# A two-layer transformer block: folded query weights, split key tables and a fourth buffer of gathered rows in the sparse attention

## The chip, the cores and the metric

The kernel runs on one core of one Trainium2 chip. The metric is the device time of one execution in microseconds, the median of the runs given. The engines are named as the profile names them: PE (TensorE matmul), PEld (its weight loads), DVE (VectorE), ACT (ScalarE), POOL (GpSimd) and SP (SyncE, which here only issues DMAs).

## The reference, cut to what matters

A sequence of 2048 rows of 128 values passes four stages, each added to the residual: a dense attention, a mixture of 16 experts, a sparse attention, and a shared expert with 8 hashed ones. Only the third is changed. Its inputs are in fact used for one sequence of 2048 rows, with at most 96 keys for each query row:

```python
c_kv = x @ W_dkv                                   # 2048 x 32
I = sum_h relu(q_i @ k_i.T) * idx_w                # index scores, 4 heads
# of row t: the last 64 keys always, later keys never, and of the rest the best
_, idx = jax.lax.top_k(I, 96)                      # 64 near keys, then 32 far ones
key_c = (c_kv @ W_uk)[idx];  value = (c_kv @ W_uv)[idx]
c_q = x @ W_dq                                     # 2048 x 64
query_c = c_q @ W_uq                               # 8 heads x 64
query_r = rotate(softplus(c_q @ W_qr))             # 8 heads x 32, angle by row
key_r = rotate(softplus((x @ W_kr)[idx]))          # angle by place in idx
attn = softmax((query_c . key_c + query_r . key_r) * scale)
out = (attn . value) @ W_out
```

## The kernel before

The rows are cut into 16 tiles of 128 (t = 0 to 15). The sparse attention, `layer1_attention`, has two blocks of instructions, and between two blocks all engines meet: none starts the next block before all have ended this one.

**The first block, `projections1`.** DVE normalizes the rows. PE then works through a list `jobs`, in a ring of four PSUM banks; each job fills one bank and ACT (for some jobs DVE) empties it. The kinds are `xnT` (four transposes of normalized rows), `kv` (the 64 numbers of each key: 32 of c_kv and 32 for the rotation), `ki` and `qi` (index keys and queries, kept as a high and a low half, the low one computed by DVE), `cq` (the 64 numbers c_q of each row), `wqq` (W_uq and W_uk folded for each head), `q` (one tile of all heads' queries, from c_q and `wqq`), `nout` (W_uv and W_out folded) and `near` (transposes of the rotated keys). Between jobs, `begin` and `finish` mark where a softplus starts and ends, and `scored` where the index scores of the first three tiles are computed and ranked (`first_score`, `first_rank`). DVE's `new_keys` adds the keys' softplus to `rows`, SP copies all of `rows` to the table `key_table` in HBM, and POOL, once the table is there and a tile is ranked (`place_ready`), gathers the far keys: each indirect DMA fetches 128 rows of 64 numbers, tile 0 has 16 of them and every other tile 32 (`gathers`). In this block POOL issues those of tiles 0 and 1, on line 1137.

**The second block, `selected_attention`.** The order of the work on PE, ACT and DVE is written out in slots by `selected_schedule`, eight slots a tile; `index_schedule` spreads the index scores and the ranking of the tiles 3 to 15 over the slots, and `A_SLOT` says how many slots the scoring of tile 0 starts behind them. Each tile needs, in this order: its gathered keys rotated in two halves on DVE (`keys`; first instruction on line 1041), their transposes on PE and copies on ACT (`far`), scores, softmax, and the context sums on PE, which read the gathered rows themselves (line 1746), then the product with `nout` and the addition to x (line 1668). `spin` rotates the queries of two tiles, on DVE with `angle` tables that SP loads; unit 0 stands at the start of this block. POOL runs on its own:

```python
for t in range(GATHERED, NT):
    m = t % RING
    pool.wait_ge(place_ready, t + 1)
    if t >= RING:
        pool.wait_ge(ctx_full, 2 * (t - RING + 1))
    for i in range(32):
        pool.indirect_dma_start(far[m][:, i, :], ...)
```

So a tile's gathers wait until the tile is ranked, and until the context sums of the tile `RING` before it, which held the same buffer, are done. A row's place list lies in one of six buffers (`PLACES`).

## Time and profile before

| what | value |
|---|---|
| median of 3 runs | 2347.01 us (2346.33 to 2355.41) |
| the profiled execution | 2350.25 us, its span 2348.5 us |
| projections, first to second meeting of the engines | 1500.9 to 1608.7 us |
| second block of the sparse attention | 1608.7 to 2281.9 us |
| PE busy over the span | 91% |
| POOL busy over the span | 78% |

The times of the views are microseconds from the start of the span. The profiled execution took 3.24 us more than the median of the runs, and 1.75 us of it lie outside its span. What happens before 1500.9 us and after 2281.9 us is the work of the other three stages.

### The profile page before, as it was taken

The numbers are of one execution on the slowest core, as the hardware profiler recorded it, in microseconds if no ns is written. First come the engines' busy times: TensorE is split into PE (matmuls) and PEld (weight loads), VectorE is DVE, ScalarE is ACT, GpSimd is POOL, SyncE is SP. The second block draws the span as 40 slices with busy tenths as digits, with TensorE's granted clock in tenths as the row PEclk, the third lists the DMA queues.
The fourth block names the chain that finished last, engine by engine and source line by source line (L and its number), as shares of the span: only waits on it lengthen the run. The fifth ranks groups of instructions, "written<-read, shape, count | busy, mean of one in ns | idle before, by whom it ended". The sixth has DMA issues, their size and how long they took to land. (4 is left out here: it accounts for less than half of the span.)

```text
span 2348.5 us, 56810 instructions
## 1 busy us (share of the span) xinstructions
PE 2136.3 (91%) x22652; PEld 1279.2 (54%) x22652; DVE 1793.4 (76%) x3458; ACT 1718.3 (73%) x3500; POOL 1825.1 (78%) x1239
## 2 busy tenths in 40 slices
PE   5899999999999999999999689787999888887868
PEld 2466666666666666666666556533454444444434
DVE  7788888888888888888887379767788777775223
ACT  4898998989989989899899546445666756654433
POOL 4899999999999999999999547357177777777700
PEclk8999999999999999999999789865689998977769
DMA  4000000000000000000000001111111111111110
GB/s 147 1 2 2 2 2 2 2 2 2 2 2 2 2 2 2 2 2 3 2 2 2 15 13 27 47 28 32 30 33 38 38 31 38 33 31 35 32 29 18
DMA packets 44288, 43.19 MB, mean 18 GB/s; under 512 B 20912, under 2 KB 33024, under 8 KB 43776
## 3 DMA queue, kind: packets, MB, share of 16 engines
q0 software_dynamic: 15872, 16.28, 3.7%
q1 hardware_dynamic: 28160, 23.35, 3.5%
q8 instruction: 178, 2.92, 0.5%
q14 instruction: 78, 0.64, 0.1%
HBM read 33.83 MB, written 1.57 MB: 15 GB/s over the span
## 5 line engine op out<-in xcount | busy, mean ns | idle before, releaser
L380 POOL TENSOR_TENSOR probs_lo<-probs,probs_hi 128x1024 f16<-128x1024 f32 x512 | 1076.4, 2127 | 41.7 <-ACT probs L430 41.2
L494 DVE TENSOR_REDUCE part_max<-aux 128x1 f32<-128x512 f32 x1024 | 677.7, 686 | 90.8 <-PE aux L568 86.4
L429 ACT ACTIVATE probs_hi<-scores 128x512 f16<-128x512 f32 x1024 | 627.9, 613 | 133.4 <-PE scores L601 116.0
L430 ACT ACTIVATE probs<-scores 128x512 f32<-128x512 f32 x1024 | 633.4, 619 | 0.0
L1509 POOL DMA_INDIRECT far<-key_table,placeT x448 | 442.7, 988 | 189.4 <-issue 135.9
L617 PE MATMUL acc<-v,probs_hi 128*128 128x65 f16 x4096 | 451.6, 193 | 2.3 <-POOL probs_lo L380 2.3
L619 PE MATMUL acc<-v,probs_hi 128*128 128x64 f16 x4096 | 452.8, 195 | 0.0
L621 PE MATMUL acc<-v,probs_lo 128*128 128x65 f16 x4096 | 451.1, 192 | 0.0
L617 PEld LDWEIGHTS acc<-v,probs_hi 128*128 128x128 f16 x4096 | 382.8, 96 | 82.7 <-POOL probs_lo L380 2.6
L619 PEld LDWEIGHTS acc<-v,probs_hi 128*128 128x128 f16 x4096 | 380.3, 97 | 75.5
L568 PE MATMUL aux<-k_a,q_a 128*128 128x512 f16 x1024 | 392.6, 384 | 4.4 <-DVE roped L480 2.1
L600 PE MATMUL scores<-q_a,k_a 128*128 128x512 f16 x1024 | 388.7, 380 | 6.6 <-ACT probs L430 6.5
L601 PE MATMUL scores<-q_b,k_b 65*128 65x512 f16 x1024 | 389.6, 380 | 0.0
L621 PEld LDWEIGHTS acc<-v,probs_lo 128*128 128x128 f16 x4096 | 381.8, 99 | 0.0
L601 PEld LDWEIGHTS scores<-q_b,k_b 65*128 65x128 f16 x1024 | 100.1, 98 | 112.5 <-issue 0.2
L568 PEld LDWEIGHTS aux<-k_a,q_a 128*128 128x128 f16 x1024 | 100.1, 98 | 83.0 <-DVE part_max L494 13.8
L600 PEld LDWEIGHTS scores<-q_a,k_a 128*128 128x128 f16 x1024 | 100.3, 98 | 81.4 <-ACT probs L430 26.1
L846 POOL TENSOR_TENSOR e_hid_lo<-e_hid,e_hid_hi 128x512 f16<-128x512 f32 x64 | 74.1, 1159 | 63.4 <-ACT e_hid_hi L802 63.4
L1041 DVE TENSOR_TENSOR far_turned<-far,cos_far 128x512 f32<-128x512 f32 x31 | 21.6, 697 | 131.9 <-DMA far<-key_table,placeT 131.8
L1528 ACT ACTIVATE farT<-a_turn 128x512 f32<-128x512 f32 x64 | 38.2, 597 | 103.5 <-PE a_turn L1699 102.9
L472 DVE TENSOR_TENSOR rope_term<-aux,cos 128x512 f32<-128x512 f32 x128 | 88.5, 691 | 25.6 <-PE aux L551 22.5
L1723 PE MATMUL a_score<-near_keys,qT 64*128 64x256 f32 x256 | 105.3, 496 | 0.0
(319 smaller groups left out, 4083.3 us busy)
## 6 DMA issues: line engine op xcount, KB each, us to landing
far<-key_table,placeT POOLq DMA_INDIRECT x496
qT<-qT SPq DMA_DIRECT2D x16, 256.0 KB
e_w<-in_e_w SPq DMA_DIRECT2D x48, 64.0 KB, 1.9
x<-in_x SPq DMA_DIRECT2D x4, 256.0 KB, 3.9
cos<-in_cos SPq DMA_DIRECT2D x1, 1024.0 KB, 7.0
sin<-in_sin SPq DMA_DIRECT2D x1, 1024.0 KB, 9.0
e_w<-in_e_w SPq DMA_DIRECT2D x2, 512.0 KB, 4.1
out<-x SPq DMA_DIRECT2D x4, 256.0 KB, 2.7
```

The costliest lines, as they stand in the source:

```text
L380: pool.tensor_tensor(probs_lo[:, slot], probs[:, wide], probs_hi[:, slot], ALU.subtract).then_inc(low_ready, 1)
L429: act.activation(probs_hi[:, slot, i], bank, ACT.Exp, scale=float(DH0) ** -0.5)
L430: act.activation(probs[:, wide, i], bank, ACT.Exp, scale=float(DH0) ** -0.5).then_inc(probs_ready, 1)
L494: dve.tensor_reduce(part_max[g % 2][:, n % QT, n // QT:n // QT + 1], bank, AX.X, ALU.max).then_inc(aux_free, 1)
L568: ins = pe.matmul(bank, qa[g % QRING][:, t * P:(t + 1) * P], ka[h % 2][:, c * CH:(c + 1) * CH], start=True, stop=True)
L600: pe.matmul(out, ka[h % 2][:, keys], qa[g % QRING][:], start=True, stop=False)
L601: pe.matmul(out, kb[h % 2][:, keys], qb[g % QRING][:], start=False, stop=True).then_inc(scores_ready, 1)
L617: pe.matmul(out, probs_hi[:, n % SLOTS, i, queries], high, start=(kt == 0 and t == 0), stop=False, skip_group_check=True)
L619: pe.matmul(out[:, 0:DH0], probs_hi[:, n % SLOTS, i, queries], low, start=False, stop=False, skip_group_check=True)
L621: ins = pe.matmul(out, probs_lo[:, n % SLOTS, i, queries], high, start=False, stop=(kt == KT0 - 1), skip_group_check=True)
L1509: pool.indirect_dma_start(far[m][:, i, :], None, keep["table"], bass.IndirectOffsetOnAxis(ap=placeT[t % PLACES][:, i:i + 1], axis=0)).then ...
L1723: pe.matmul(b[:, 0:WIN], qT[t % 2][0:KW, 0, 4 * g:4 * g + 4].rearrange("k i a h -> k (i a h)"), near[:, t * P:t * P + WIN], start=False, s ...
```

## The change

In words, part by part:

- **Buffers.** `RING` is 4: there is a fourth buffer `far3`. It is paid for in memory by laying `nout` and the context sums `ctxT` on the 32 partitions beside the near keys (`BESIDE`), and by keeping `near_key` in `far3` during the first block.
- **POOL.** The first block issues the first 32 gathers only (16 of tile 0, 16 of tile 1) and reads a table of the first 1024 rows; the second block issues the other 464.
- **Key tables.** The keys are finished and written in two halves, each with its own softplus, and the near keys are rotated later, by `near_keys`.
- **Projections.** The four `cq` jobs go. One job `wall` multiplies W_dq into `wqq`, and each `q` job multiplies 128 rows of weights with the transposed x. `wqq` and `nout` come before the first `xnT`, behind six loads of their own (`fold_in`). ACT empties all `q` jobs (DVE emptied every other one). The list `after` says what follows which job.
- **First rotation.** `spin` 0 moves to the first block (`first_spin`), its `angle` loads with it.
- **Slots.** `A_SLOT` is 2.

```diff
-RING = 3
+RING = 4
 EARLY = 3
-GATHERED = 2
+FIRST_GATHERS = 2 * 16
+FIRST_ROWS = T // 2
 TOP_OPS = 3 * (FAR // 8)
+ANGLES = ("cos_q", "sin_q", "cos_near", "sin_near")
...
+        wdqT = sb("wdqT", [CQ, D], F32)
         wuq = sb("wuq", [DH1, H1, CQ], F32)
         wuk = sb("wuk", [DH1, H1, CKV], F32)
         wuv = sb("wuv", [DH1, H1, CKV], F32)
         wo = sb("a1_wo", [DH1, H1, D], F32)
...
-        wqq = sb("wqq", [CQ, H1 * CKV + NQ], F32)
+        wqq = sb("wqq", [CQ, H1, ROPE1 + CKV], F32)
+        wq_all = sb("wq_all", [P, H1 * (ROPE1 + CKV)], F32)
...
-        near_key = sb("near_key", [P, NT, KW], F32)
-        last_e, last_u = (part[:, NT - SOFT:].rearrange("p t h r -> p (t h r)") for part in (e, u))
+        near_key = keep["far"][RING - 1][:, 0:NT, :]
+        last_e = e[:, NT - SOFT:].rearrange("p t h r -> p (t h r)")
...
-        jobs = [("xnT", c) for c in range(NCH)] + [("kv", i) for i in range(2)]
+        folded = [(wuq, "wuq"), (wuk, "wuk"), (wuv, "wuv"), (wo, "a1_wo"), (wqq[:, :, 0:ROPE1], "wqr"), (wdqT, "wdqT")]
+        loads = [(wkvr, "wkvr"), (widxk, "widxk"), (widxq, "widxq"), (keep["idx_w"], "idx_w"),
+                 (keep["cap0"], "cap0"), (keep["cap"], "cap"), (cos_k, "cos_k"), (sin_k, "sin_k"),
+                 (keep["mask"], "mask_first"), (keep["unit"], "unit"), (keep["cos_far"], "cos_far"),
+                 (keep["sin_far"], "sin_far")]
+
+
+
         later = [i for i in range(NIDX * NCH) if i % NCH]
-        jobs += [("ki", 0)] + [("qi", NCH * h) for h in range(NIDX)] + [("ki", c) for c in range(1, NCH)]
-        jobs += [("cq", c) for c in range(NCH)] + [("wqq", 0)] + [("q", t) for t in range(NT)]
-        jobs += [("qi", i) for i in later]
-        jobs += [("nout", i) for i in range(2)] + [("near", c) for c in range(NCH)]
-        by_vector = lambda kind, i: kind in ("ki", "qi") or (kind == "q" and i % 2 == 1)
+        queries = lambda lo, hi: [("q", t) for t in range(lo, hi)]
+        jobs = [("wqq", 0), ("nout", 0), ("nout", 1), ("xnT", 0), ("ki", 0), ("qi", 0), ("xnT", 1), ("qi", NCH),
+                ("kv", 0), ("qi", 2 * NCH), ("qi", 3 * NCH), ("xnT", 2), ("xnT", 3), ("wall", 0), ("kv", 1), ("ki", 1)]
+        jobs += queries(0, 3) + [("ki", 2)] + queries(3, 8) + [("ki", 3)] + queries(8, NT)
+        jobs += [("qi", i) for i in later] + [("near", c) for c in range(NCH)]
+        by_vector = lambda kind, i: kind in ("ki", "qi")
...
+        after = {
+            ("kv", 0): [("begin", 0)],
+            ("qi", 3 * NCH): scores(0),
+            ("xnT", 3): [("finish", 0), ("rank", 0)],
+            ("kv", 1): [("begin", 1)],
+            ("ki", 1): scores(1) + [("finish", 1)],
+            ("q", 0): [("rank", 1)],
+            ("ki", 2): scores(2),
+            ("q", 3): [("begin", 2), ("rank", 2)],
+            ("q", 5): [("near", 0)],
+            ("q", 7): [("begin", 3)],
+            ("q", 8): [("finish", 2)],
+            ("q", 9): [("spin", 0)],
+            ("q", 11): [("begin", 4), ("finish", 3)],
+            ("q", 15): [("begin", 5)],
+            ("qi", later[2]): [("finish", 4)],
+            ("qi", later[6]): [("finish", 5)],
+        }
...
+                for dst, src in folded:
+                    sp.dma_start(dst if isinstance(dst, bass.AP) else dst[:], dram[src]).then_inc(fold_in, 16)
                 for dst, src in loads:
-                    sp.dma_start(dst if isinstance(dst, bass.AP) else dst[:], dram[src]).then_inc(w_in, 16)
-                sp.wait_ge(keep["rows_ready"], 1)
-                sp.dma_start(keep["table"].rearrange("(t p) d -> p t d", p=P), rows[:]).then_inc(keep["table_out"], 16)
-                sp.wait_ge(keep["table_out"], 16)
+                    sp.dma_start(dst[:], dram[src]).then_inc(w_in, 16)
+                for k in range(2):
+                    for j, n in enumerate(ANGLES):
+                        sp.dma_start(angle[k][:, j], dram[n][:, SPIN * k:SPIN * k + SPIN, :]).then_inc(angles_in[k], 16)
+                for k in range(2):
+                    sp.wait_ge(rows_ready, k + 1)
+                    sp.dma_start(keep["table"][k * FIRST_ROWS:(k + 1) * FIRST_ROWS, :].rearrange(
+                        "(t p) d -> p t d", p=P), rows[:, of_keys(k), :]).then_inc(table_out[k], 16)
+                for k in range(2):
+                    sp.wait_ge(table_out[k], 16)
...
-                pool.wait_ge(keep["table_out"], 16)
-                for t in range(GATHERED):
-                    pool.wait_ge(place_ready, t + 1)
-                    for i in range(gathers(t)):
-                        pool.indirect_dma_start(far[t][:, i, :], None, keep["table"],
-                                                bass.IndirectOffsetOnAxis(ap=placeT[t][:, i:i + 1], axis=0)
-                                                ).then_inc(far_in[t][i // 16], 16)
+                pool.wait_ge(table_out[0], 16)
+                for t, i in gather_list()[:FIRST_GATHERS]:
+                    if i == 0:
+                        pool.wait_ge(place_ready, t + 1)
+                    pool.indirect_dma_start(far[t][:, i, :], None, keep["table"][0:FIRST_ROWS, :],
+                                            bass.IndirectOffsetOnAxis(ap=placeT[t][:, i:i + 1], axis=0)
+                                            ).then_inc(far_in[t][i // 16], 16)
 
             @block.scalar
             def _(act):
@@ -1158,44 +1186,43 @@
...
-                def new_keys():
-                    dve.wait_ge(mu_ready, 1)
-                    dve.tensor_copy(rows[:, :, CKV:], mu_k[:]).then_inc(keep["rows_ready"], 1)
-
-                    dve.wait_ge(w_in, len(loads) * 16)
+                def new_keys(k):
+                    dve.wait_ge(mu_ready, k + 1)
+                    dve.tensor_copy(rows[:, of_keys(k), CKV:], mu_k[:, of_keys(k)]).then_inc(rows_ready, 1)
+
+                def near_keys():
+                    dve.wait_ge(mu_ready, 2)
                     own.mark(dve.tensor_copy(near_key[:, :, ROPE1:], rows[:, :, 0:CKV]))
-                    rotate(dve, own, near_key[:, :, 0:ROPE1], mu_k[:], cos_k[:], sin_k[:], soft("e", 0), soft("u", 0)
+                    rotate(dve, own, near_key[:, :, 0:ROPE1], mu_k[:], cos_k[:], sin_k[:], key_e[:], key_u[:]
                            ).then_inc(near_ready, 1)
+
+                def first_spin():
+                    dve.wait_ge(angles_in[0], 4 * 16)
+                    dve.wait_ge(near_ready, 2)
+                    dve.wait_ge(mu_ready, 3)
+                    mu_q = QN[:, 0:SPIN, :, 0:ROPE1]
+                    buffers = [ap[:].rearrange("p (t h) r -> p t h r", t=SPIN) for ap in (key_e, key_u)]
+                    for i, first in enumerate((ROPE1 + CKV, 0)):
+                        cos, sin = (angle[0][:, 2 * i + j].unsqueeze(2).broadcast_to([P, SPIN, H1, ROPE1])
+                                    for j in range(2))
+                        if i:
+                            dve.wait_ge(queries_ready, 1)
+                        rotate(dve, own, QN[:, 0:SPIN, :, first:first + ROPE1], mu_q, cos, sin, *buffers
+                               ).then_inc(queries_ready, 1)
 
...
                             ins = mm(b[0:CQ, h * CKV:(h + 1) * CKV], wuq[:, h, :], wuk[:, h, :])
+                    elif kind == "wall":
+                        pe.wait_ge(free, free_no["wqq", 0])
+                        ins = mm(b[:], wdqT[:], wqq[:].rearrange("p h c -> p (h c)"))
                     elif kind == "q":
-                        ins = mm(b[:], cqT[:, i * P:(i + 1) * P], wqq[:])
+                        pe.wait_ge(free, free_no["wall", 0])
+                        ins = mm(b[:], xnT[:, i * P:(i + 1) * P], wq_all[:])
                     elif kind == "ki":
...
-A_SLOT = 3
+A_SLOT = 2
...
-    work += [("spin", k, 0)] if j == -2 or (j + 3 + NG) % (NG * SPIN) == 0 and 0 < k < NT // SPIN else []
+    work += [("spin", k, 0)] if (j + 3 + NG) % (NG * SPIN) == 0 and 0 < k < NT // SPIN else []
...
+def gather_list():
+
+    return [(t, i) for t in range(NT) for i in range(gathers(t))]
+
...
-                for t in range(GATHERED, NT):
+                for t, i in gather_list()[FIRST_GATHERS:]:
                     m = t % RING
-                    pool.wait_ge(place_ready, t + 1)
-                    if t >= RING:
-                        pool.wait_ge(ctx_full, 2 * (t - RING + 1))
-                    for i in range(32):
-                        pool.indirect_dma_start(far[m][:, i, :], None, keep["table"],
-                                                bass.IndirectOffsetOnAxis(ap=placeT[t % PLACES][:, i:i + 1], axis=0)
-                                                ).then_inc(far_in[m][i // 16], 16)
+                    if i == 0:
+                        pool.wait_ge(place_ready, t + 1)
+                        if t >= RING:
+                            pool.wait_ge(ctx_full, 2 * (t - RING + 1))
+                    pool.indirect_dma_start(far[m][:, i, :], None, keep["table"],
+                                            bass.IndirectOffsetOnAxis(ap=placeT[t % PLACES][:, i:i + 1], axis=0)
+                                            ).then_inc(far_in[m][i // 16], 16)
 
...
+        near_keys = sb("near_keys", [P, P + T], F32)
+        beside = lambda n: near_keys[BESIDE, n * H1 * D:(n + 1) * H1 * D].rearrange("c (h d) -> c h d", h=H1)
         keep = {
             "rows": sb("rows", [P, NT, KW], F32),
             "queries": sb("queries", [P, NT, H1, QW], F32),
-            "near_keys": sb("near_keys", [KW, P + T], F32),
-            "nout": sb("nout", [CKV, H1, D], F32),
+            "near_keys": near_keys[0:KW, :],
+            "nout": beside(0),
+            "ctxT": beside(1),
             "qi": sb("qi", [P, NIDX, T], F16),
```

The order on POOL, from its last row of the experts on. Before (the numbers behind the names are those of the buffers):

```order
L1137 DMA far0<-key_table,placeT0 128x64 [waits a1_place_ready,table_out]
L1137 DMA far0<-key_table,placeT0 128x64 x15
L1137 DMA far1<-key_table,placeT1 128x64 [waits a1_place_ready]
L1137 DMA far1<-key_table,placeT1 128x64 x31
L1122 UNCONDITIONAL_BRANCH
L1501 UNCONDITIONAL_BRANCH [waits barrier_Pool_Activation_PE_DVE_SP_gather]
L1509 DMA far2<-key_table,placeT2 128x64 [waits a1_place_ready]
L1509 DMA far2<-key_table,placeT2 128x64 x31
L1509 DMA far0<-key_table,placeT3 128x64 [waits a1_ctx_full,a1_place_ready]
L1509 DMA far0<-key_table,placeT3 128x64 x31
L1509 DMA far1<-key_table,placeT4 128x64 [waits a1_ctx_full,a1_place_ready]
```

and with the change:

```order
L1165 DMA far0<-key_table,placeT0 128x64 [waits a1_place_ready,table_out0]
L1165 DMA far0<-key_table,placeT0 128x64 x15
L1165 DMA far1<-key_table,placeT1 128x64 [waits a1_place_ready]
L1165 DMA far1<-key_table,placeT1 128x64 x15
L1142 UNCONDITIONAL_BRANCH
L1548 UNCONDITIONAL_BRANCH [waits barrier_Pool_Activation_PE_DVE_SP_gather]
L1556 DMA far1<-key_table,placeT1 128x64 x16
L1556 DMA far2<-key_table,placeT2 128x64 [waits a1_place_ready]
L1556 DMA far2<-key_table,placeT2 128x64 x31
L1556 DMA far3<-key_table,placeT3 128x64 [waits a1_place_ready]
L1556 DMA far3<-key_table,placeT3 128x64 x31
L1556 DMA far0<-key_table,placeT4 128x64 [waits a1_ctx_full,a1_place_ready]
```

Of tile 1, 16 gathers move behind the meeting of the engines, and tile 3 no longer waits for `ctx_full`; the first to do so is tile 4.

The order on PE at the start of the first block. Before:

```order
L1288 UNCONDITIONAL_BRANCH [waits barrier_Pool_Activation_PE_DVE_SP_release]
L1302 MATMUL a1_bank0<-ident,softplus_u 128x128 [waits a1_normed]
L1302 MATMUL a1_bank0<-ident,softplus_u 128x128 x3
L1302 MATMUL a1_bank1<-ident,softplus_u 128x128 [waits a1_normed]
L1302 MATMUL a1_bank1<-ident,softplus_u 128x128 x3
L1302 MATMUL a1_bank2<-ident,softplus_u 128x128 [waits a1_normed]
L1302 MATMUL a1_bank2<-ident,softplus_u 128x128 x3
L1302 MATMUL a1_bank3<-ident,softplus_u 128x128 [waits a1_normed]
L1302 MATMUL a1_bank3<-ident,softplus_u 128x128 x3
L1298 MATMUL a1_bank0<-wkvr,a1_xnT 128x64 [waits a1_free,a1_w_in]
L1298 MATMUL a1_bank0<-wkvr,a1_xnT 128x64 x7
```

and with the change:

```order
L1334 UNCONDITIONAL_BRANCH [waits barrier_Pool_Activation_PE_DVE_SP_release]
L1344 MATMUL a1_bank0<-wuk,wuq 64x32 [waits a1_fold_in]
L1344 MATMUL a1_bank0<-wuk,wuq 64x32 x7
L1344 MATMUL a1_bank1<-a1_wo,wuv 32x128 x4
L1344 MATMUL a1_bank2<-a1_wo,wuv 32x128 x4
L1349 MATMUL a1_bank3<-ident,softplus_u 128x128 [waits a1_normed]
L1349 MATMUL a1_bank3<-ident,softplus_u 128x128 x3
L1344 MATMUL a1_bank0<-a1_xnT,widxk 128x512 [waits a1_w_in,a1_free]
L1344 MATMUL a1_bank1<-a1_xnT,widxq 128x512 [waits a1_free]
L1349 MATMUL a1_bank2<-ident,softplus_u 128x128 [waits a1_normed,a1_free]
L1349 MATMUL a1_bank2<-ident,softplus_u 128x128 x3
L1344 MATMUL a1_bank3<-a1_xnT,widxq 128x512 [waits a1_free]
```

The two folds of weights stand ahead of the first transpose, and the first product that needs all loads (`a1_w_in`) has three of the four `xnT` jobs behind it instead of before it.

The order on DVE where the near keys are rotated, with the change (before, the rotation stood between the first and the second `qi` of the block):

```order
L1279 STREAM_TRANSPOSE placeT<-first_place 128x32 [waits a1_own]
L1239 COPY far<-rows 128x16x32 [waits a1_mu_ready]
L1044 TENSOR_TENSOR softplus_key_e<-mu_k,cos_k 128x512
L1047 TENSOR_TENSOR softplus_key_u<-mu_k,sin_k 128x16x16
L1048 TENSOR_TENSOR softplus_key_u<-mu_k,sin_k 128x16x16
L1050 TENSOR_TENSOR far<-softplus_key_e,softplus_key_u 128x16x32 [waits a1_own]
L1309 TENSOR_SCALAR softplus_u<-softplus_e 128x1024 [waits a1_e_ready]
L1311 SCALAR_TENSOR_TENSOR softplus_e<-softplus_u,softplus_e 128x1024 [waits a1_own]
L1299 TENSOR_TENSOR ki_lo<-a_bank,ki_hi 64x512 [waits a1_hi_ready]
```

Between the ranking of tile 2 (ended by STREAM_TRANSPOSE) and the low half of the last `ki` now stand the key rotation and half of a softplus. The first rotation of the queries follows 4 rows later, ahead of the remaining `qi`.

## Rows read from the trace of the kernel before

**Rows 1.** The page: busy time and instructions of each engine

```profile
PE 2136.3 (91%) x22652; PEld 1279.2 (54%) x22652; DVE 1793.4 (76%) x3458; ACT 1718.3 (73%) x3500; POOL 1825.1 (78%) x1239
```

**Rows 2.** Windows: us, busy PE PEld DVE ACT POOL, clock, DMA share, GB/s

```profile
1500.90:1608.70 107.80, 83.97 (x200) 37.98 (x201) 70.81 (x190) 51.09 (x91) 48.11 (x48) 0.64 0.17 43
1608.70:1699.80 91.10, 80.67 (x394) 35.56 (x394) 73.33 (x155) 53.36 (x112) 32.39 (x33) 0.59 0.14 34
1699.80:1846.30 146.50, 133.97 (x1018) 72.93 (x1018) 121.86 (x230) 102.79 (x240) 112.15 (x113) 0.93 0.18 35
1846.30:2236.60 390.30, 324.69 (x2371) 178.36 (x2368) 241.63 (x425) 226.43 (x526) 298.15 (x303) 0.84 0.18 34
```

**Rows 3.** Timeline of POOL: start, duration, what; idle before it

```profile
1603.50 0.95 POOL L1137 DMA_INDIRECT far<-key_table,placeT  x1 [0.30 <-issue]
1609.32 0.94 POOL L1509 DMA_INDIRECT far<-key_table,placeT  x1 [4.88 <-POOLq L1122]
...
1699.76 0.94 POOL L1509 DMA_INDIRECT far<-key_table,placeT  x1 [48.65 <-PE a_ctx L1746]
...
2235.64 0.94 POOL L1509 DMA_INDIRECT far<-key_table,placeT  x1 [0.31 <-issue]
```

**Rows 4.** Waits of 1609 to 2260 us: in total, times, longest

```profile
DVE far_turned L1041 <- DMA far<-key_table,placeT: 131.8, 20, 12.5
...
POOL far L1509 <- PE a_ctx L1746: 48.6, 1, 48.6
```

**Rows 5.** Timeline of DVE: first wait for rows, last half tile, end

```profile
1846.33 0.69 DVE L1041 TENSOR_TENSOR far_turned<-far,cos_far 128x512 f32<-128x512 f32 x1 [2.03 <-DMA far<-key_table,placeT]
...
2238.12 0.69 DVE L1041 TENSOR_TENSOR far_turned<-far,cos_far 128x512 f32<-128x512 f32 x1 [12.09 <-DMA far<-key_table,placeT]
...
2281.35 0.29 DVE L1668 TENSOR_TENSOR x<-x,a_turn 128x128 f32<-128x128 f32 x1 [19.55 <-PE a_turn L1705]
```

**Rows 6.** Timeline of PE: context sums of tile 0, the second half

```profile
1697.30 1.70 PE L1746 MATMUL a_ctx<-a_probsT,far 128*32 128x32 f32 x32
```

**Rows 7.** Timeline of DVE: the place list of tile 15

```profile
2145.59 0.19 DVE L1606 STREAM_TRANSPOSE placeT<-place 128x32 uint32<-128x32 uint32 x1
```

**Rows 8.** Windows of two tiles at the full clock

```profile
1811.00:1846.00 35.00, 31.41 (x260) 17.03 (x257) 30.72 (x54) 26.20 (x60) 26.77 (x28) 1.00 0.17 34
1846.00:1882.00 36.00, 30.79 (x246) 16.44 (x243) 26.45 (x48) 25.41 (x58) 27.47 (x29) 1.00 0.19 37
```

**Rows 9.** Groups of PE in the first block

```profile
L1298 PE MATMUL a_bank<-wqq,cqT 64*128 64x512 f32 x32 | 26.4, 1019 | 0.5 <-ACT wqq L1180 0.5
...
L1298 PE MATMUL a_bank<-a_xnT,a_wdq 128*64 128x512 f32 x8 | 7.2, 1028 | 0.0
L1302 PE MATMUL a_bank<-ident,softplus_u 128*128 128x128 f32 x16 | 4.2, 435 | 8.7 <-DVE softplus_u L98 8.7
...
L1298 PE MATMUL a_bank<-a_wo,wuv 64*32 64x128 f32 x16 | 1.9, 270 | 1.9 <-DVE qi L1262 1.9
...
L1298 PE MATMUL a_bank<-wuk,wuq 64*64 64x32 f32 x16 | 1.1, 220 | 0.0
```

**Rows 10.** Timeline of PE: first index scores, an index key product

```profile
1533.65 0.22 PE L1334 MATMUL first_bank<-ki_hi,qi 128*128 128x96 f16 x1 [5.34 <-DVE qi L1262]
...
1535.33 2.07 PE L1298 MATMUL a_bank<-a_xnT,widxk 128*128 128x512 f32 x2
1537.19 0.37 PE L1334 MATMUL first_bank<-ki_hi,qi 128*128 128x192 f16 x1
```

**Rows 11.** Timeline of DVE: key rotation, query rotation, each with what follows

```profile
1529.57 0.68 DVE L1041 TENSOR_TENSOR softplus_key_e<-mu_k,cos_k 128x512 f32<-128x512 f32 x1
...
1531.68 1.91 DVE L1262 TENSOR_TENSOR qi<-a_bank,qi 64x512 f16<-64x512 f32 x3
...
1616.31 0.68 DVE L1041 TENSOR_TENSOR far_turned<-queries,angle 128x512 f32<-128x512 f32 x1
...
1620.67 0.69 DVE L1041 TENSOR_TENSOR far_turned<-far,cos_far 128x512 f32<-128x512 f32 x1
```

198 lines of the change are left out of this document (95 added, 103 removed).

## The prediction

> **What bounds the kernel now.** I first split the span at the meetings of the engines. Only the stretch from 1500.9 to 2281.9 us is touched, so the question is what sets its length. The page shows PE busy for 91% of the span [rows 1], which tempts one to call the kernel PE-bound. The windows [rows 2] show that this is a mean over stretches with different limits: in the last long one (1846.3 to 2236.6) PE is busy 324.69 of 390.30 us (83%), DVE 62%, ACT 58%, POOL 298.15 (76%).
>
> POOL's own timeline tells why 76% is in truth 100%: each of its rows there is idle for only 0.30 us, "issue", and busy for 0.94 [rows 3]. The gathers of one tile follow each other without a wait. Of the 496 gathers (16 and 15 x 32), 48 are issued in the first block and 32, those of tile 2, right after the second meeting. Then POOL stands for 48.65 us, and what it waits for is line 1746 on PE, the context sums of tile 0 [rows 3, 4], which end at 1697.30 + 1.70 = 1699.00 [rows 6]. After it POOL goes from 1699.76 to 2235.64 without another wait: 13 tiles, 416 gathers, 415 steps in 535.88 us, which is 1.2913 us for a step and 41.3 us for a tile. Everything else follows it: DVE waits for gathered rows 20 times, 131.8 us in all, up to 12.5 us at a time [rows 4], the first at 1846.33 and the last at 2238.12 [rows 5]. Behind the last gather the work of the last half tile takes 2281.35 - 2235.64 = 45.7 us [rows 3, 5]. So the end of the stage is POOL's last gather plus a tail, and POOL's last gather is set by one wait near the beginning.
>
> Why does POOL's 48.65 us wait for a buffer bound the end when nobody waits for rows until 1846.33? Because POOL is slower than the rest: where PE has its full clock, a tile takes 35 or 36 us, with PE busy 31 of it [rows 8]; POOL needs 41.3. A lead that POOL loses early is missed later.
>
> **The second block with the change.** POOL has 464 gathers there instead of 448: 463 steps x 1.2913 = 597.9 us from its first to its last, if it never waits. Before, this took 2235.64 - 1609.32 = 626.32 us [rows 3]. The difference is -28.4 us: the wait of 48.65 us goes, and 16 x 1.29 = 20.7 us come, because 16 gathers move into this block. Does it never wait? Tile 3 needs no context sums now. Tile 4 waits for those of tile 0. Its first gather is number 16 + 32 + 32 = 80 of the block, 103.3 us after the start; the sums of tile 0 ended 1699.00 - 1609.32 = 89.7 us after it. That leaves 13.6 us, and tile 0 should be earlier rather than later, since the first rotation (4.36 us [rows 11]) has left the block ahead of it. For tiles 5, 6 and on, each needs 41.3 us more on POOL's side and 35 to 39 on PE's, so the margin grows. The place lists: the last was ready at 2145.59 [rows 7], 536.3 us after the start; its tile now starts at gather 432, 557.9 us. `A_SLOT` 2 instead of 3 moves the index work a slot (some 5 us) either way; 21.6 us cover it.
>
> The price of a gather I leave at 1.2913. The queue could be shared differently with four buffers, but DMA share is 0.18 [rows 2], and a step was 0.94 + 0.30 before and behind the wait [rows 3].
>
> The tail of 45.7 us stays, if the rest has caught up with POOL by then. This is the step with the most risk. The first wait for rows stood at 237.0 us after the start (1846.33 - 1609.32). It was for the first half of tile 6, whose last row with the change is fetched by gather 16 (rest of tile 1) + 4 x 32 (tiles 2 to 5) + 16 = 160 of the block, at 159 x 1.2913 = 205.3 us, plus 2.5 to land and be read (2238.12 - 2235.64 [rows 3, 5]). The other engines, if no faster than before up to there, are 237.0 - 207.8 = 29 us behind POOL and have 9.5 tiles to make it good. At full clock they gain 41.3 - 35 = 6.3 us a tile and are there in 29/6.3 = 4.6 tiles, around tile 11. To be there only at the end they may take 41.3 - 29/9.5 = 38.3 us a tile. At the clock of before in that stretch, 0.84 [rows 2], PE's busy time is 324.69/9.5 = 34.2 us a tile, and the time beside it at full clock is 35 - 31.41 = 3.6 or 36 - 30.79 = 5.2 [rows 8], which gives 38 to 39: just the deadline. But I read the 0.84 as the effect of PE's standing for rows: in tiles without such waits it was 1.00 [rows 8]. So I expect 1.00 until they have caught up, and the waits for rows to begin late.
> The Trainium skill ("TensorE: Matmul & The Clock Gate", section on HAM oscillation) says the same of the cause: waits for a DMA between bursts of matmuls take PE back to its lower clock. By that rule the change, with fewer such waits, has a faster PE; the trace agrees as far as 1.00 without waits against 0.84 with them goes, and the sum does not use it.
>
> **The projections.** They end with a meeting, and PE has most of the work: 83.97 of 107.80 us at clock 0.64 [rows 2]. Terms:
> - Four `cq` jobs go: -7.2 [rows 9]. One job `wall` of the same form as one `q` comes: +1.7 (26.4/16 = 1.65 [rows 9]).
> - 16 `q` jobs have weights of 128 rows instead of 64. By durations nothing changes (1028 ns with 128 rows, 1019 with 64 [rows 9]): bound 0. By the pitch, two matmuls with 128-row weights took 1537.19 - 1535.33 = 1.86 [rows 10] against 1.65: +3.4. I take +2.5, nearer to the pitch, since PE there goes job after job.
> - `wqq` and `nout` (1.1 + 1.9 us, and waits of 0.5 and 1.9 [rows 9]) move to the start, where PE waits 8.7 us for DVE's normalized rows [rows 9]: -5.4. Cover: 8.7 us of layer norm; if their six loads come late, they cost their 3.0 again.
> - The first index scores waited 5.34 us for DVE's `qi` [rows 10], and 2.1 of them were the rotation of the near keys (1529.57 to 1531.68 [rows 11]), which now comes later: -2.5, between 0 and -5.3.
> - Three of the four `xnT` jobs now stand behind the first product that needs all loads, and no longer beside the layer norm's end: 12/16 of 4.2 [rows 9], +3.1 (bounds 0 and 3.1).
> - DVE's chain grows by the rotation of the queries (4.36 us [rows 11]) ahead of the last `qi`, which fill PE's banks; DVE loses 8 of the `q` copies, ACT has them all, and it was busy 51.09 of 107.80 [rows 2]. +2.5, bounds 0 and 4.7.
>
> The sum is -7.2 + 1.7 + 2.5 - 5.4 - 2.5 + 3.1 + 2.5 = **-5.3 us**, bounds about -12 and +3.
> On the 128-row weights the Trainium skill ("TensorE: Matmul & The Clock Gate", Part 2, step LDWEIGHTS) holds that loading depends on the columns and that the number of rows does not matter. By it the third term is 0 and the sum -7.8; by the pitch it is -5.3, and no row here has both forms side by side.
>
> What POOL still does in this block, 32 gathers, began no earlier than tile 0's ranking and ended at 1603.50 with 48; with 32 it is done 16 x 1.29 = 20.7 us sooner. So POOL cannot hold the meeting, and its second block begins 5 us earlier with the rest.
>
> **Sum.** -28.4 - 5.3 = -33.7, rounded with the small margins to -33.3. On the profiled execution: 2350.25 - 33.3 = 2317. It was 3.24 us over the median, so against the median 2347.01 - 33.3 = **2313.7 us**.
>
> **The rivals.**
> - *PE (not POOL) is the bound to the end.* If the clock does not stay at 1.00, the 29 us are not caught up. Before, the stretch from the first wait (237.0) to the last (2238.12 - 1609.32 = 628.8) went at 391.8/9.5 = 41.2 us a tile; at a pace p the block changes by 9.5 x (p - 41.2). At 40 us a tile that is -11.4, with the projections -16.7: 2330 us. It decides from 38.3 up. For it: 0.59 and 0.64 in the two stretches before [rows 2], in one of which nobody waited for rows. Against it: 0.93 and 1.00 after 1699.8 [rows 2, 8], where the work of a tile is as it will be. Chance 0.15.
> - *The wait is only moved.* POOL stands at tile 4 (its margin is 13.6 us) or at a place list, or the projections grow by what the block saves. The gain of 28 is used up if the sums of tile 0 come 13.6 + 28 = 42 us later than now. In the trace they do not: nothing is put ahead of tile 0 on PE. 2342, or 2350 with projections at their upper bound and some of the tail; chance 0.06.
> - *Slower: PE near half clock through the stage.* PE's busy time a tile was 31.1 us at clock 1.00 and 34.2 at 0.84 [rows 2, 8], 19 us more for each 1.0 of clock lost. At 0.60 it would be 39, with 4.5 beside it 43.4 a tile: 9.5 x 2.2 = 21 us more than before, less 5.3: 2347 + 15.6 = 2363 us. It decides from a pace of 43.0 (a mean clock of 0.62). For it speaks 0.59 in the stretch up to 1699.8, where PE was busy 80.67 of 91.10 us, more than in the projections, and nobody waited for rows [rows 2]; against it, that the work of the later tiles had 0.93 and 1.00 [rows 2, 8]. Chance 0.03.
>
> **How the numbers follow.** POOL-bound to the end, 2300 to 2325: 0.76. The first rival 0.15, the second 0.06, the third 0.03. The likeliest one's range is 2313.7 with -12 + 5.3 and +3 + 5.3 of the projections, 2307 to 2322, and 3 us either side for the level between executions. The range for 8 in 10 takes in most of the first rival: 2303 to 2333. A change of 0.5% is 12 us, about what a measurement of this kernel can tell from none: faster by more than that 0.91 (all of the first case and nearly all of the first rival), within it 0.06, slower 0.03.
>
> **What would show it.** In the changed kernel's trace: POOL has 464 gathers in the second block, without a wait for `ctx_full` of more than a few us, and first to last is 598 us. Its wait on line 1746 is gone and not replaced by one on a ranking. DVE's waits for rows add up to less than half of 131.8 us, and begin around tile 11 (near 413 us after the block's start, gather 320) and not at tile 6. PE's clock is near 1.00 in tiles 5 to 10. The projections take 102.5 us (96 to 111). The tail from the last gather is 45.7 us; if it is much longer, the first rival has won. I am wrong if a gather's step isn't 1.29 any more, if the start of the second block runs at the half clock for longer, or if the projections lose more by their new order than the jobs that are gone.

## The result and the profile after

The changed kernel takes 2318.23 us (median of 5 runs, 2315.02 to 2318.90), the kernel before 2348.24 us (5 runs). The ratio is 0.9865, 95% interval 0.9849 to 0.9881: 1.35% faster. The forecast was 2313.7 us, -33.3 us; measured are -30.0 us between the medians and -32.0 us between the two profiled executions (2350.25 and 2318.22 us).

The answers to [rows 1 to 3], for the changed kernel. First the page:

```profile
PE 2114.8 (91%) x22646; PEld 1271.2 (55%) x22646; DVE 1788.0 (77%) x3447; ACT 1732.7 (75%) x3506; POOL 1829.3 (79%) x1239
```

The windows of the first block, of the same 91 us behind the meeting, up to the first wait for gathered rows, and on to the last gather:

```profile
1499.10:1598.70 99.60, 68.54 (x194) 34.11 (x194) 69.52 (x187) 61.09 (x97) 33.72 (x32) 0.73 0.16 44
1598.70:1689.80 91.10, 83.34 (x444) 40.35 (x444) 70.87 (x152) 56.33 (x119) 69.58 (x69) 0.70 0.18 44
1689.80:2038.30 348.50, 320.16 (x2353) 170.50 (x2352) 285.49 (x507) 246.30 (x562) 266.72 (x268) 0.90 0.16 35
2038.30:2201.90 163.60, 130.23 (x982) 73.23 (x980) 76.77 (x143) 83.85 (x198) 125.04 (x127) 0.80 0.15 33
```

POOL's timeline, the first gather of all, the first and the last of the second block:

```profile
1538.68 1.10 POOL L1165 DMA_INDIRECT far<-key_table,placeT  x1 [41.85 <-DVE placeT L1286]
1599.47 0.94 POOL L1556 DMA_INDIRECT far<-key_table,placeT  x1 [17.63 <-POOLq L1142]
...
2200.92 0.94 POOL L1556 DMA_INDIRECT far<-key_table,placeT  x1 [0.30 <-issue]
```

The waits of 1599 to 2225 us, the answer to [rows 4] (in total, times, longest), and the rows of DVE that answer to [rows 5]:

```profile
POOL far L1556 <- issue: 140.7, 462, 0.3
...
DVE far_turned L1044 <- DMA far<-key_table,placeT: 76.3, 9, 13.3
...
POOL far L1556 <- PE a_ctx L1793: 0.3, 1, 0.3
```

```profile
2038.36 0.69 DVE L1044 TENSOR_TENSOR far_turned<-far,cos_far 128x512 f32<-128x512 f32 x1 [0.80 <-DMA far<-key_table,placeT]
...
2203.28 0.69 DVE L1044 TENSOR_TENSOR far_turned<-far,cos_far 128x512 f32<-128x512 f32 x1 [13.27 <-DMA far<-key_table,placeT]
...
2249.36 0.29 DVE L1715 TENSOR_TENSOR x<-x,a_turn 128x128 f32<-128x128 f32 x1 [19.62 <-PE a_turn L1752]
```

The reader sees three things. POOL's wait of 48.65 us is gone, and nothing took its place: what is left between two gathers is "issue", 0.3 us each. POOL is still the bound at the end, since DVE waits for its rows up to 13.3 us at a time. And the others are not held by it until 2038.36, 439 us into the block, where before it began at 237 us.

I cut the profiled executions at DVE's first row of the first block (1501.09 before, 1499.28 after), at POOL's first and last gather of the second block, and at the end of the last addition to x:

| stretch | before | after | difference | forecast |
|---|---|---|---|---|
| ahead of the first block | 1501.09 | 1499.28 | -1.8 | none |
| first block, up to POOL's first gather of the second | 108.23 | 100.19 | -8.0 | -5.3 |
| POOL, first to last gather | 626.32 | 601.45 | -24.9 | -28.4 |
| last gather to the last addition | 46.00 | 48.73 | +2.7 | 0 |
| all three | 780.55 | 750.37 | -30.2 | -33.7 |

The stretch ahead of the block holds the same work in all kernels here and lasted from 1495.20 to 1501.09 us in their profiles: its -1.8 us is no part of the change, and the three stretches are what experiments are compared by below.

### The profile page after: what moved, and what is told of

The parts are those of the page before. It is cut to its first block and busy times, and to the rows that moved or that the text cites. A ratio compares the mean times of both kernels' runs of the same rounds, so it can differ in the third digit from the quotient of the medians.

```text
span 2316.4 us, 56818 instructions
## 1 busy us (share of the span) xinstructions
PE 2114.8 (91%) x22646; PEld 1271.2 (55%) x22646; DVE 1788.0 (77%) x3447; ACT 1732.7 (75%) x3506; POOL 1829.3 (79%) x1239
## 5 line engine op out<-in xcount | busy, mean ns | idle before, releaser
L1556 POOL DMA_INDIRECT far<-key_table,placeT x464 | 461.3, 994 | 158.7 <-issue 140.7
L1680 DVE SCALAR_TENSOR_TENSOR index<-relu,idx_w,index 128x512 f32<-128x512 f32 (+4 forms) x111 | 72.7, 655 | 44.1 <-ACT relu L1595 40.9
```

The costliest lines, as they stand in the source:

```text
L1556: pool.indirect_dma_start(far[m][:, i, :], None, keep["table"], bass.IndirectOffsetOnAxis(ap=placeT[t % PLACES][:, i:i + 1], axis=0)).then ...
```

## Experiments

Ratios are against the kernel before in the same rounds; the changed kernel's is 0.9865, from rounds of its own. Where less than 0.3% matters, I use the stretches of the profiles. They scatter too: runs 3, 4 and 10, whose edits left all three stretches nearly alone, have 746.61, 747.64 and 746.35 us in sum where the changed kernel's profile has 750.37. So a difference of up to some 4 us between two profiles says nothing.

**1. Wait as with three buffers.**

```diff
-                        if t >= RING:
-                            pool.wait_ge(ctx_full, 2 * (t - RING + 1))
+                        if t >= RING - 1:
+                            pool.wait_ge(ctx_full, 2 * (t - RING + 2))
```

> Four buffers stay, but each tile's gathers wait for the context sums of the tile three before it, as with three buffers. In the profile of the changed kernel the context sums of tile 0 end 76.9 us after POOL's first gather of the block, those of tiles 1 and 2 at 120.6 and 164.3. My theory (POOL sets the end, so each of its waits is paid in full): tile 3 would start at 62.4 and waits 15 us, tiles 4 and 5 wait 2 to 3 us each, about +20 us: 2338 us, POOL's idle time on the context sums 18 to 22 us. First rival (all of the gain is the fourth buffer, the rest gives nothing): 2343 to 2346 us. Second rival (POOL is not the bound in the changed kernel, the other engines are): the wait is there but the time stays at 2318 to 2323 us.

Measured: 2332.35 us, ratio 0.9952 (0.9936 to 0.9968). POOL's first to last gather takes 620.91 us (+19.5), the three stretches 769.76 us (+19.4), DVE waits 96.4 us. The first of POOL's waits, and their sum:

```profile
1678.00 0.94 POOL L1556 DMA_INDIRECT far<-key_table,placeT  x1 [18.19 <-PE a_ctx L1793]
```

```profile
POOL far L1556 <- PE a_ctx L1793: 23.9, 4, 18.2
```

The forecast +20 us is met by the stretches and by the ratio (+0.0087, 20 us); the medians alone give +14 against the changed kernel and +16 against runs 3 and 4 of the same rounds. A wait of POOL near the beginning is paid about in full 500 us later. Both rivals are out, by some 10 us each in the median. It also shows that the fourth buffer is not all of it: with three, this wait is 18.19 us and not 48.65, because 16 more gathers (20.8 us) lie ahead of it and the context sums of tile 0 are there 12.8 us sooner after POOL's start (76.9 instead of 89.7).

**2. 48 gathers in the first block.**

```diff
-FIRST_GATHERS = 2 * 16
+FIRST_GATHERS = 3 * 16
```

> The first block issues 48 gathers again, all of tiles 0 and 1. POOL's work in the second block shrinks by 16 x 1.30 = 20.8 us; in the first it would end near 1600.5 us instead of 1579, so the meeting comes some 2 to 3 us later. My theory (POOL sets the end only because the others caught up at tile 11; unhindered they took (438.9 - 235.8)/5.5 = 36.9 us a tile): the last half tile can be reached 17 us earlier, net -14.6 us: 2304 us, DVE's waits for gathered rows below 30 us. Rival 1 (the other engines are already the bound, the tail is theirs): 2318 to 2321 us. Rival 2 (POOL-bound throughout, the others follow at any pace): 2300 us.

Measured: 2302.70 us, ratio 0.9823 (0.9797 to 0.9849). The first block takes 110.61 us (+10.4), POOL's part of the second 580.86 (-20.6), the three stretches 739.21 (-11.2). DVE waits for rows 4 times, 43.0 us. POOL around the meeting:

```profile
1602.17 0.94 POOL L1165 DMA_INDIRECT far<-key_table,placeT  x1 [0.30 <-issue]
1607.99 0.94 POOL L1556 DMA_INDIRECT far<-key_table,placeT  x1 [4.88 <-POOLq L1142]
```

and PE's first row behind it:

```profile
1607.39 0.53 PE L1813 MATMUL a_idx<-ki_hi,qi 128*128 128x448 f16 x1 [11.14 <-PEq L1142]
```

POOL is now what the others wait for at the meeting: PE stands 11.14 us there, and 0.94 in the changed kernel. The 4.88 us before POOL's row are thus what the meeting itself takes when POOL comes last. The same 4.88 stands in the kernel before [rows 3], which has the same 48 gathers; what follows from that is said with run 11. That cost 10.4 us and not the 2 to 3 I gave it (in the stretches -11.2 where I gave -14.6). In the second block all of the 20.6 us were gained and not 17, and the last 4 half tiles still wait for POOL: there the second rival's mechanism is right. The first rival is out. The first block, 110.61 us, is even 2.4 us longer than before the change (108.23): with 48 gathers in it nothing is left of what the new order of the projections saves.

**3. The first rotation back in the second block.**

```diff
-            ("q", 9): [("spin", 0)],
...
-    work += [("spin", k, 0)] if (j + 3 + NG) % (NG * SPIN) == 0 and 0 < k < NT // SPIN else []
+    work += [("spin", k, 0)] if j == -2 or (j + 3 + NG) % (NG * SPIN) == 0 and 0 < k < NT // SPIN else []
```

> The first rotation of the queries stands in the second block again, ahead of the first keys. My theory: in the first block it costs DVE 4.3 us ahead of the copies of qi, which PE waits for, and in the second it is hidden, since the others wait for POOL later anyway: 2.5 to 4.2 us faster, 2314 to 2316 us, the first block 2.5 to 4.2 us shorter and POOL's first to last gather unchanged at 601 us. Rival (taking it out of the second block is part of the gain): 4.3 us slower, 2322.5 us, or no change of the sum, 2318 us, where both sides are on the path.

Measured: 2316.67 us, ratio 0.9885 (0.9861 to 0.9909); first block 100.37 us (+0.2), POOL 599.96 (-1.5), the first wait for rows 438.6 us after the start (438.9 in the changed kernel). The rotation is hidden in either place: the block is no shorter without it, against my 2.5 to 4.2 us. The intervals of the two ratios overlap, and no stretch shows the 4.3 us of the rival, whose 2318 us for "no change of the sum" fits as well as my 2314 to 2316.

**4. 64 rows of weights in the q products.**

```diff
-                        ins = mm(b[:], xnT[:, i * P:(i + 1) * P], wq_all[:])
+                        ins = mm(b[:], xnT[0:CQ, i * P:(i + 1) * P], wq_all[0:CQ, :])
```

> The q products use 64 of the 128 rows of their weights and of the transposed x (half of the sum is left out), all else is the same. My price of the longer weights, 0.155 us for each of 16 products: 2.5 us faster, 2315.7 us, the pitch of two matmuls 0.15 us lower at the same clock. Rival (the rows of the weights cost nothing): 2318 us, and the same duration and pitch of each product.

Measured: 2316.77 us, ratio 0.9888 (0.9857 to 0.9919); first block 101.17 us. The groups of the q products on PE in the first block, in the changed kernel and then with 64 rows (busy us, mean ns, idle before):

```profile
L1344 PE MATMUL a_bank<-wq_all,a_xnT 128*128 128x512 f32 x32 | 20.0, 781 | 9.3 <-DVE ki_lo L1299 9.3
```

```profile
L1344 PE MATMUL a_bank<-wq_all,a_xnT 64*128 64x512 f32 x32 | 28.5, 1069 | 3.6 <-DVE ki_lo L1299 3.6
```

Neither theory foresaw this: with half the rows they take 8.5 us *more*. (The expectation of run 8 gives 26.8 us for them; the trace has 28.5.) The first six matmuls, up to which the two traces agree, with 128 rows and with 64:

```profile
1539.77 5.49 PE L1344 MATMUL a_bank<-wq_all,a_xnT 128*128 128x512 f32 x6
```

```profile
1539.78 5.38 PE L1344 MATMUL a_bank<-wq_all,a_xnT 64*128 64x512 f32 x6
```

The difference is 0.02 us for each matmul: the price of long weights is as good as nothing. What differs is the clock. The window 1541 to 1585 in the kernel before, the changed one, and this one (the last column but two is the granted clock):

```profile
1541.00:1585.00 44.00, 43.53 (x77) 15.96 (x77) 28.40 (x73) 21.16 (x41) 32.93 (x34) 0.58 0.11 24
```

```profile
1541.00:1585.00 44.00, 26.92 (x52) 10.53 (x52) 35.31 (x76) 32.81 (x45) 31.70 (x31) 0.81 0.12 29
```

```profile
1541.00:1585.00 44.00, 39.87 (x51) 13.32 (x50) 33.44 (x73) 31.42 (x43) 31.33 (x31) 0.52 0.13 30
```

And the block is only 1.0 us longer for it: most of PE's 8.5 us more are taken from its wait for DVE (9.3 to 3.6) and from others. In the changed kernel PE's work does not bound this block.

**5 to 8. A chip on which engines stood for long with no partner in the trace.** The next four ran together on another chip, where the kernel before took 2797.21 us.

> The changed kernel itself once more, on the chip and in the rounds of the three that follow, so that they can be compared with it. Every theory expects the ratio of before, 0.9865 (0.985 to 0.988).

> The first block issues 40 gathers instead of 32 (tile 0 and 24 of tile 1). In the changed kernel's trace POOL waited 17.63 us at the meeting, of which 4.9 are the meeting itself; 8 gathers at 1.33 us are 10.6 us and fit into the other 12.7. With 48 (the run before) they did not: the first block grew by 10.4 us, the block behind it shrank by 20.6. My theory (POOL's chain of 496 gathers sets the end, a gather is free where POOL would stand at the meeting): first block unchanged at 100.2 us, POOL's part of the second shorter by 8 x 1.296 = 10.4 us, 0.9865 - 0.0044 = 0.982. Rival (the others could not use it): 0.9865.

> In the first block DVE ranks tile 2 and rotates the near keys after the low half of the last index keys instead of ahead of it. In the changed kernel's trace PE stood 9.31 us for that low half. My theory now (DVE's chain ahead of that copy bounds the first block, PE no longer does since its q products had clock 0.79): the wait on PE falls to below 3 us and the first block gets 4 to 9 us shorter, ratio 0.983 to 0.985. Rival (the sum of DVE's and ACT's work sets the block, the wait comes back before the last qi copies): first block shorter by 0 to 2 us, ratio 0.9865, and other waits of PE on DVE and ACT grow by what this one loses.

> The kernel before, but its 16 q products take 128 rows (the transposed x and the index weights stand in for c_q and the folded weights, so the queries are other numbers); everything else, the cq jobs too, stays. In the changed kernel the 32 matmuls of q took 20.0 us at clock 0.79 of that stretch, before 26.4 at 0.58, and with 64 of the 128 rows left out 26.8 at 0.50. Theory A (128 rows in place of 64 bring the granted clock up): the 32 take 20 to 22 us instead of 26.4, and the first block gets 3 to 6 us shorter, ratio 0.997 to 0.9985. Theory B (the order of jobs and the waits brought the clock up): they take 26 to 28 us, ratio 1.000 to 1.001.

Their edits: run 5 has none, run 6 has `FIRST_GATHERS = 40`; run 7 is

```diff
-            ("q", 3): [("begin", 2), ("rank", 2)],
-            ("q", 5): [("near", 0)],
+            ("q", 3): [("begin", 2)],
...
-            ("q", 8): [("finish", 2)],
+            ("q", 8): [("finish", 2), ("rank", 2), ("near", 0)],
```

and run 8 is the kernel before with

```diff
-                        ins = mm(b[:], cqT[:, i * P:(i + 1) * P], wqq[:])
+                        ins = mm(b[:], xnT[:, i * P:(i + 1) * P], widxq[:])
```

Measured: the changed kernel 2791.02 us, ratio 0.9983 (0.9969 to 0.9996); 40 gathers 0.9972 (0.9953 to 0.9990); late ranking 0.9987 (0.9968 to 1.0005); before with 128 rows 1.0002 (0.9988 to 1.0015). Run 8's theory B named just that ratio (1.000 to 1.001), but no expectation of a time could be tested here: the first blocks alone took 114.51, 117.83, 111.35 and 134.29 us in place of 100 and 108. The waits in the second block for the changed kernel here, and the same wait of POOL in run 8:

```profile
POOL far L1556 <- PE a_ctx L1793: 380.6, 11, 68.8
DVE biggest L1710 <- remote: 213.4, 22, 29.2
ACT farT L1575 <- remote: 181.3, 12, 70.5
```

```profile
POOL far L1509 <- PE a_ctx L1746: 445.9, 13, 73.1
```

Engines stand for up to 72 us with no partner in the profile ("issue", "remote"). What held them stays open: no view of the trace names it and no run tests it. It has a place, though. DVE's first row of the first block stands at 1495.2 to 1499.2 us in these four profiles, as on the other chips, so all of the extra time comes behind it. POOL, which was never held by the context sums in the changed kernel's own profile, waits for them at 11 tiles, some 35 us each. So POOL is not the bound here, as in the first rival of the prediction, though it is not PE's pace that holds the others; and the price is nearly the whole gain: 1.35% becomes 0.17%.

**9. 40 gathers in the first block, again,** on a third chip, since POOL was not the bound in any of the last four runs.

> [...] My theory as before: first block 100.2 us from its first row of DVE to POOL's first gather of the second, POOL's first to last gather 601.45 - 10.4 = 591 us, ratio 0.982. Rival (the others could not use it): 0.9865.

Measured: 2307.10 us, ratio 0.9836 (0.9821 to 0.9851). First block 100.09 us (-0.1), POOL 591.32 (-10.1), the three stretches 739.76 (-10.6). POOL waited 5.93 us at the meeting instead of 17.63. Against run 10, from the same rounds and with 32 gathers, it is -8.9 us on POOL, -6.6 in the three stretches and -7.0 between the medians. The eight gathers were free where they went, as expected. 48 and 40 gathers come to the same, 739.2 and 739.8 us: behind the point where POOL holds the meeting nothing more is won, since all 496 gathers stand in one chain.

**10. Late ranking, again** (the edit of run 7).

> [...] My theory: the wait of 9.31 us on PE falls to below 3 us, the first block is 4 to 9 us shorter than 100.2, ratio 0.983 to 0.985. Rival (DVE's and ACT's work sets the block): 0 to 2 us shorter, ratio 0.9865, other waits of PE on DVE and ACT longer by what this one loses.

Measured: 2314.08 us, ratio 0.9871 (0.9854 to 0.9888), first block 99.96 us (-0.2). PE's groups in the first block:

```profile
L1343 PE MATMUL a_bank<-a_xnT,widxq 128*128 128x512 f32 x32 | 20.3, 780 | 15.0 <-DVE qi L1303 11.0 <-ACT queries L1205 4.0
L1343 PE MATMUL a_bank<-wq_all,a_xnT 128*128 128x512 f32 x32 | 17.3, 689 | 2.5 <-DVE ki_lo L1298 2.5
```

The rival is right about the time. The wait of 9.3 us fell to 2.5, and the one ahead of the last index queries rose from 7.4 in sum to 15.0. A stall on an engine that has time is not a price. That DVE's and ACT's work sets the block, as the rival has it, is not shown by this.

**11. The kernel before with 128 rows, again** (the edit of run 8).

> The kernel before with q products of 128 rows (transposed x times index weights in place of c_q times the folded ones, so other queries), again. Theory A (128 rows in place of 64 bring the granted clock up): the 32 matmuls take 20 to 22 us instead of 26.4, and the first block gets 3 to 6 us shorter than 108.2. Theory B (the order of jobs and waits brought the clock up in the changed kernel): 26 to 28 us, the block as before.

Measured: 2345.34 us, ratio 0.9988 (0.9974 to 1.0002). The q products and the window, the answers to 26.4 us [rows 9] and to 0.58 above:

```profile
L1298 PE MATMUL a_bank<-widxq,a_xnT 128*128 128x512 f32 x32 | 15.3, 612 | 3.6 <-DVE queries L1267 3.0 <-ACT wqq L1180 0.5 <-ACT queries L1180 0.2
```

```profile
1541.00:1585.00 44.00, 35.73 (x83) 12.41 (x82) 35.48 (x79) 28.17 (x48) 33.53 (x35) 0.85 0.11 26
```

Theory A holds for the clock, more than expected: 15.3 us. (The values that are multiplied differ here too; in run 4 they are the changed kernel's own, and it goes the same way.) For the time it fails: the first block is 107.06 us, only 1.2 shorter, and the ratio cannot be told from 1. PE's last two rows of the block, its first of the next, and POOL's rows beside them tell why:

```profile
1589.97 1.93 PE L1298 MATMUL a_bank<-a_wo,wuv 64*32 64x128 f32 x16 [1.77 <-DVE qi L1262]
1593.91 3.22 PE L1324 MATMUL a_bank<-ident,near_key 128*64 128x128 f32 x16 [2.01 <-DVE qi L1262]
1605.62 0.53 PE L1766 MATMUL a_idx<-ki_hi,qi 128*128 128x448 f16 x1 [8.50 <-PEq L1122]
```

```profile
1600.40 0.94 POOL L1137 DMA_INDIRECT far<-key_table,placeT  x1 [0.30 <-issue]
1606.22 0.94 POOL L1509 DMA_INDIRECT far<-key_table,placeT  x1 [4.88 <-POOLq L1122]
```

PE ends its part 97.97 us after DVE's first row, and 105.76 in the kernel before: 7.8 us sooner, for 11.1 us less of work. It then stands 8.50 us at the meeting, because POOL's 48 gathers are not issued yet. The 1.2 us that the block did gain are POOL's own: its last gather starts 101.24 us after DVE's first row instead of 102.41. So this run does not say that PE's work counts for nothing in the kernel before. It says that POOL holds the meeting there, and that what PE saves is lost waiting for it.

**12. Tile 0 ranked earlier, with 40 gathers.**

```diff
-            ("xnT", 3): [("finish", 0), ("rank", 0)],
+            ("xnT", 3): [("rank", 0), ("finish", 0)],
```

> 40 gathers in the first block, and DVE ranks tile 0 before it finishes the softplus of the first keys instead of after. In the changed kernel's trace DVE stood 3.5 us for ACT ahead of that softplus, which the ranking (4.8 us) can fill; the key table then leaves some 1.5 us later. My theory (POOL's chain of 496 gathers sets the end, so it counts from when its first one can go): first gather 37 to 38 us after the first row of DVE instead of 39.4, time 1.5 to 2.5 us below the run with 40 gathers alone. Rival (the table is last): no earlier, or up to 1 us later.

Measured: 2304.26 us, ratio 0.9825 (0.9809 to 0.9841). The first gather:

```profile
1536.49 1.10 POOL L1165 DMA_INDIRECT far<-key_table,placeT  x1 [41.26 <-DMA key_table<-rows]
```

That is 38.82 us after DVE's first row (1497.67), against 39.84 in run 9 and 39.40 in the changed kernel, and it now waits for the table and no more for the places. One microsecond is gained, not two, and it bought nothing: POOL waits 7.86 us at the meeting instead of 5.93. The three stretches are 735.90 us, 3.9 below run 9, of which 2.2 are a shorter tail (46.16 against 48.35) and 1.8 a shorter step of the gathers (1.296 against 1.300), both within what these two vary by between all profiles; the intervals of the ratios overlap. Either version, and that of run 2, beats the changed kernel's 750.37 us by over 10 us, and the 746.35 to 747.64 of runs 3, 4 and 10 by 6.6 to 11.7.

## Why the prediction was right, point by point

**POOL sets the end: right, and shown.** Adding a wait (run 1, +19.4 us for +19.5 on POOL) and taking gathers away (run 9, -10.6 for -10.1) both moved the end by what they moved POOL, within the scatter (with the medians +14 to +16 and -7 to -11 us).

**The second block, -28.4: the term came to -24.9.** No wait replaced the one of 48.65 us, as worked out. Two sizes were off. A step took 601.45 / 463 = 1.299 us and not 1.291, which is 3.6 us, all of the miss. Without POOL's waits it ranged from 1.291 to 1.300 in the ten profiles on undisturbed chips, so that is scatter and not a cost of the change. The margin of tile 4, which enters no sum, was 28 us and not 13.6 (its gathers began 104.97 us after POOL's first), mostly because tile 0's sums came 12.8 us sooner.

**The tail, 0: it was +2.7.** It is 46.0 us before and 48.7 after, but in the other profiles it takes 48.7, 47.7, 46.3, 48.7, 48.4, 46.2, 48.3 and 46.2 us, and of these 48.3 is the kernel before with 128 rows. It is no effect of the change.

**The catching up: right in place, wrong in clock.** The first wait for rows came in tile 11, as forecast (439 us after the start against 413). The pace of the tiles 6 to 11 was (438.9 - 235.8) / 5.5 = 36.9 us where I took 35, and the clock from 1835.3 to 2038.3 us 0.93 where I took 1.00. So the step that read 0.84 as the effect of waits for rows alone was too simple: the window from 1689.8 to 2038.3 has no such wait and 0.90. The reading under it was wrong too. I called the windows of [rows 8] tiles without such waits, but in the second, 1846 to 1882 us, DVE waits for rows twice, 2.03 and 5.59 us, and the clock is 1.00. The last stretch of the changed kernel, with such waits, has 0.80. The Trainium skill ("TensorE: Matmul & The Clock Gate", section on HAM oscillation) has it that they lower the clock; the last stretch agrees with this in its direction, the window of 1846 to 1882 us does not, and they are not all that lowers it. What else did stays open. DVE's waits fell to 76.3 us; I had said below half of 131.8, which would be 65.9. The last tiles have little left to do beside the rows they wait for, and in each of the last four half tiles some 13 us of wait are left.

**The projections, -5.3: -8.0, and not for the reasons given.** This is the part of the prediction that failed in its working. It took PE as the bound ("PE has most of the work"), summed PE's jobs, and asked of POOL only whether it could hold the meeting *with* the change. It can't, as worked out, but before the change it did. There POOL's wait at the meeting is the bare 4.88 us, as in runs 2 and 11, where PE stands 11.14 and 8.50 us for it. In the kernel before PE stands 1.87 us, where 0.94 is enough with POOL out of the way. So two chains ended within about 1 us of each other, and the gain needs both parts of the change:
- The 16 gathers that left the block took POOL's chain away. Alone that is worth about 0.9 us (1.87 - 0.94, an estimate); without it the rest is worth nothing (run 2).
- The other engines' chain got shorter. PE's last matmul of the block ends 98.65 us after DVE's first row, and 105.76 before: -7.1. With the 0.9 this is the measured 8.0.

What bounds that other chain is only partly shown. In the kernel before PE's work counts (run 11: 11.1 us less of it, PE's end 7.8 us sooner). In the changed kernel it does not: 8.5 us more on PE change the block by 1.0 us (run 4), a stall of 9.3 us moved changes it by 0.2 (run 10), and the first rotation off DVE by 0.2 (run 3). ACT, which now empties all `q` jobs, was touched by no run. The prediction's sum of jobs on one engine holds only as long as that engine stays the bound, and here it did not. Its terms' own lower bounds also add up to -16.2 us and not to the "about -12" given; -8.0 lies inside either. Term by term:
- 128-row weights, +2.5: about +0.02 us a matmul, and the clock rose. The rule of the Trainium skill ("TensorE: Matmul & The Clock Gate", step LDWEIGHTS), that the rows of the weights do not matter, is what the first six matmuls show; the rule says nothing of the clock, which over 1541 to 1585 us was 0.81 to 0.85 with 128 rows and 0.52 to 0.58 with 64.
- The first rotation, up to +4.7: nothing (run 3).
- The first index scores, -2.5: their wait for `qi` fell from 5.34 to 3.3 us, so the size was about right, but it did not bring the last `qi` forward.
- The `cq` jobs, -7.2: up to the last `qi` nothing of them is left. From DVE's first row to its end on PE it took 96.4 us before and 96.6 after, though PE was busy 15.4 us less in the block (68.54 against 83.97): what its work lost, its waits gained. No run takes the `cq` jobs away alone.
- `wqq` and `nout` to the start, -5.4: here lies the gain of the second chain, but at the other end of the block. These are the last rows of PE in it, before and after:

```profile
1591.62 5.83 PE L1298 MATMUL a_bank<-a_xnT,widxq 128*128 128x512 f32 x8 [0.64 <-DVE qi L1262]
1599.31 1.93 PE L1298 MATMUL a_bank<-a_wo,wuv 64*32 64x128 f32 x16 [1.86 <-DVE qi L1262]
1603.25 3.60 PE L1324 MATMUL a_bank<-ident,near_key 128*64 128x128 f32 x16 [2.01 <-DVE qi L1262]
1608.72 0.53 PE L1766 MATMUL a_idx<-ki_hi,qi 128*128 128x448 f16 x1 [1.87 <-PEq L1122]
```

```profile
1594.76 1.13 PE L1344 MATMUL a_bank<-a_xnT,widxq 128*128 128x512 f32 x2 [1.40 <-DVE qi L1304]
1595.73 2.20 PE L1379 MATMUL a_bank<-ident,far 128*64 128x128 f32 x16
1598.87 0.35 PE L1813 MATMUL a_idx<-ki_hi,qi 128*128 128x448 f16 x1 [0.94 <-PEq L1142]
```

From the last `qi` product (1597.45) to the next block it took 11.3 us before, with `nout`, two waits for DVE, slow transposes and 0.9 us of waiting for POOL; now it takes 3.0 (1595.89 to 1598.87). That is 8.3 us, of which 7.4 are `nout`, the waits and the transposes. It is read from two traces and no run isolates it. The cover that I named for the folds at the start was only partly there: their loads landed late, PE waited 7.3 us for them and the first transpose stood at +11.2 us after DVE's first row, before at +7.2. Whether that had a price no run shows.

So the sum of that block was near the truth by luck, by errors that cancelled, and the whole forecast was carried by the one term that runs show: POOL's wait.

## What to carry to other kernels

Count the engine that is never idle in the last long stretch, find its last idle time, and look for its cause far ahead: here it was one wait for a buffer, which ended 536 us before POOL's last gather, and undoing it gave back its length to within 4 us. At a meeting of the engines, look at what each of them waits there: an engine whose wait is the shortest that it has in any run came last and holds the meeting, however much work another has done. A term may be summed on an engine only after it is shown that this engine bounds its block; otherwise a stall on it, and even its clock, can be worth nothing. Where an engine will be the bound later and stands still now, move its work forward up to the point at which it holds the next meeting, and no further (40 gathers, not 48).
